# Loading the second attention's first keys one stage earlier

## The chip, the cores and the metric

The kernel runs on one core of a Trainium2 chip. Its metric is the device time of one execution in microseconds, the median of several. Five engines work side by side, each through its own list of instructions in order: TensorE (PE; its weight loads are listed as PEld), VectorE (DVE), ScalarE (ACT), GpSimd (POOL) and SyncE (SP), which here issues nearly all DMA transfers. They wait for one another by semaphores only.

## The reference, cut to what matters

Two layers, each with a cross-attention and a mixture of experts, each added to x. x has 4 x 256 tokens of 256 numbers:

```python
x = x + L0_xattn(layernorm(x), ctx, pos, ...)      # 32 heads of 8, rotary
x = x + L0_ffn(layernorm(x), ...)                  # 16 experts, 2 a token, and a shared one
x = x + L1_xattn(layernorm(x), ctx, ...)           # 16 heads of 16, normed q and k
x = x + L1_ffn(layernorm(x), ...)                  # 60 experts, 4 a token, and a shared one

# in L1_xattn:
q = ln((x @ Wq + bq).reshape(b, s1, H, HD), qn_w, qn_b)
k = ln(kv[..., :HD], kn_w, kn_b)                   # from ctx alone: it does not depend on x
p = softmax(einsum('bhqd,bhkd->bhqk', q, k) * SCALE)
# in L0_ffn:
routed = sum over e of combine[:, e] * (relu(x @ w_up[e]) ** 2 @ w_down[e])
```

The keys of the second attention come from the context, so they can be made before x is there; the queries can't.

## The kernel before, in words

The stages follow each other and are parted by barriers of all engines: preparation and first attention (to 194 us of the profiled span), first experts (to 370 us), second attention (to 494 us), routing and shared expert of the second layer, then its routed experts with a ring of weight slots, then the sum and the store.

**The expert stage** (`route_and_experts_l0`) runs 32 passes n: 16 experts for the first 512 tokens, then the same 16 for the other 512. In each pass TensorE computes the hidden values of pass n+1 (L1041), then the outputs of pass n (L1052); ScalarE applies Relu (L1245), GpSimd squares (L1141), VectorE weighs and adds to `xs` (L1392, four tiles). The outputs of pass n wait for the square of pass n, the square for the Relu. SyncE loads the weights of one expert into one of four slots after the outputs that read it (L1427).

Between these, in chosen passes, each engine works for the second attention. All keys and the queries of the first 512 tokens are projected, normalised, turned and split into three bf16 parts whose sum is the fp32 number. ScalarE makes the first part (`high`, L1457), VectorE the remainder (`rest`, L1467), ScalarE the second part (`mid`, L1477), VectorE the third (`low`, L1486). SyncE writes the parts to stacks in DRAM (`split_writes`, L233; three transfers a split). The four key splits are written behind the expert loads of passes 20, 21, 23 and 24 (`KEYS_WRITTEN`), the two query splits behind the last pass. In passes 28 and 29 the code reads, on ScalarE and on VectorE:

```python
if n == 28:
    for s in Q_SPLITS[0:2]: high(s)     # VectorE: rest(s)
if n == 29:
    for s in Q_SPLITS[0:2]: mid(s)      # VectorE: low(s)
```

In each pass ScalarE's Relu stands ahead of these, and on VectorE the four additions of the pass do. In passes 2, 5, 8, 11, 14 and 17 SyncE also loads weights of two experts of the second layer into the first half of its ring: `ew13` (0.7 MB) and the down weights `ew2` (`load_weights`, L1760). The second half of the ring is loaded in the routing stage.

**The second attention** (`attention` with `L1`) goes through 8 units of 8 heads. A unit needs a side of keys and a side of queries, 96 rows of 8 x 256 bf16 numbers, 384 KB each, loaded from the stacks by `load_side` (L469) into one of four buffers, and rows of ones under the keys, loaded by GpSimd (`load_ones`, L488). `load_first_units` loads the first four units at the start of the stage, key side and query side in turn; one semaphore for each buffer counts both sides, and the first scores of a unit (L629) wait for it. Ahead of the loop, scores and maxima (L769) of two units run, in between the same query work for the last 512 tokens (`LateQueries`), which starts on VectorE with the norm of four tiles (L157 to L165).

Of the kernel before, what the change touches and what calls it, by code (L numbers as in the profile page):

```python
# [14 lines left out]
BF16 = mybir.dt.bfloat16  # L15
# [194 lines left out]
SB = 4  # L210
KEYS_WRITTEN = (20, 21, 23, 24)
SPLIT_BANKS = (6, 7, 0, 1)
SPLIT1_BANKS = (6, 7, 6, 7, 6, 7, 6, 7)
# [702 lines left out]
def route_and_experts_l0(nc, m, io):  # L916

    with ExitStack() as ctx:
# [42 lines left out]
        def _(sp):  # L961
# [19 lines left out]
            for n in range(UNITS0 - WSLOTS):  # L981
                sp.wait_ge(e_down_ps, 4 * (n + 1))
                load_expert_l0(sp, m, io, (n + WSLOTS) % E0, n % WSLOTS)
                if n % 3 == 2 and n // 3 < PAIRS:
                    load_weights(sp, m, io, n // 3 * 2)
                if n in KEYS_WRITTEN:
                    written(KEYS_WRITTEN.index(n))
            for s in Q_SPLITS[0:2]:
                written(s)
# [116 lines left out]
        @block.gpsimd  # L1106
        def _(pool):
            nc.gpsimd.memset(ctxT_dca[:], 0.0).then_inc(ctx_step, 1)
            pool.wait_ge(ctx_step, 1)
# [35 lines left out]
        def _(act):  # L1145
# [67 lines left out]
            def queries(n):  # L1213
# [20 lines left out]
                if n == 28:  # L1234
                    for s in Q_SPLITS[0:2]:
                        high(s)
                if n == 29:
                    for s in Q_SPLITS[0:2]:
                        mid(s)
# [10 lines left out]
        def _(dve):  # L1250
# [96 lines left out]
            def queries(n):  # L1347
# [32 lines left out]
                if n == 28:  # L1380
                    for s in Q_SPLITS[0:2]:
                        rest(s)
                if n == 29:
                    for s in Q_SPLITS[0:2]:
                        low(s)
# [247 lines left out]
def load_first_units(nc, m, io, block):  # L1633

    lay = L1
    part_dma = m.part_dma[lay.name]

    @block.sync
    def _(sp):
        for a in range(SB):  # L1640
            sp.wait_ge(part_dma[a], 16 * WRITES)
        load_side(sp, m, lay, m.ks1, "k", m.loaded1, 0, 0)
        for a in range(2):
            sp.wait_ge(part_dma[a], 2 * 16 * WRITES)
        load_side(sp, m, lay, m.qs1, "q", m.loaded1, 0, 0)
        for u in range(1, UNIT_BUFS[lay.name]):
            load_side(sp, m, lay, m.ks1, "k", m.loaded1, u, u)
            load_side(sp, m, lay, m.qs1, "q", m.loaded1, u, u)

    @block.gpsimd  # L1650
    def _(pool):
        load_ones(pool, m, io, lay, m.ks1)

# [99 lines left out]

def load_weights(eng, m, io, b):

    w13, w2, s = ring_slot(m, b)
    sem = m.ew_loaded[b % RING // 2]
    for w, dram in ((w13, "L1_w13"), (w2, "L1_w2")):
        eng.dma_start(w[:, s:s + 2, :, :].rearrange("p a c n -> p a (c n)"), io[dram][b:b + 2, :, :].rearrange(  # L1760
            "a p n -> p a n")).then_inc(sem, 16)
# [32 lines left out]
def route_shared_l1(nc, m, io, block, ctx):  # L1794
# [45 lines left out]
    def _(sp):  # L1840
# [15 lines left out]
        sp.wait_ge(xn_ready, NT)  # L1856
        sp.dma_start(m.x_rows.rearrange("(i p) d -> p i d", p=P), m.xn[:]).then_inc(m.x_sent, 16)
        for q in range(PAIRS, RING // 2):
            load_weights(sp, m, io, 2 * q)
# [484 lines left out]
def build(nc, io, out):  # L2344
    with ExitStack() as ctx:
# [12 lines left out]
        m.ew13 = m.sb("ew13", [P, EARLY, KD, 2 * I1])  # L2358
        m.ew2 = m.sb("ew2", [HCP, EARLY, 2, D])
        m.ew_loaded = [m.sem(f"ew_loaded{j}") for j in range(RING // 2)]  # L2360
# [11 lines left out]
        with ExitStack() as scope:  # L2372
# [14 lines left out]
            m.old_sems, m.stage_sems = m.stage_sems, []  # L2387
            with ExitStack() as early:
                m.qw = m.sb("qw", [P, KD + 1, D], ctx=early)
                with ExitStack() as layer:  # L2390
# [6 lines left out]
                with ExitStack() as stage:  # L2397
                    m.qs1, m.ks1 = (m.sb(n, stack_shape(L1), BF16, stage) for n in ("l1_qs", "l1_ks"))
                    m.loaded1 = [m.sem(f"l1_loaded{b}", stage) for b in range(UNIT_BUFS[L1.name])]
                    with nc.Block() as block:  # L2400
# [75 lines left out]
```

## Time and profile before

| what | us |
|---|---|
| median of 3 runs (762.67 to 765.81) | 764.84 |
| the profiled execution's own time | 768.52 |
| its span, first to last instruction | 766.6 |
| expert stage, barrier to barrier | 193.9 to 370.1 |
| second attention, barrier to barrier | 370.1 to 494.4 |
| TensorE busy in the span | 646.2 |
| VectorE busy | 425.9 |
| ScalarE busy | 297.3 |
| GpSimd busy | 259.2 |

Times on the trace's line count from the first instruction of the span. A busy share is a mean over stages with different limits, so each stage is read by itself: who waits, and for whom.

### The profile page before, as it was taken

Reading aid. Unit: us, or ns where it says so; the run is one execution under the profiler, and the core shown is the slowest. Engines: PE = TensorE matmul, PEld = TensorE weight load, DVE = VectorE, ACT = ScalarE, POOL = GpSimd, SP = SyncE. Lnnn points to the kernel's source line nnn. Section 1 sums busy time; section 2 is a strip of 40 time slices with the busy share of each in tenths; the row PEclk is TensorE's granted clock in tenths of the full one; section 3 lists DMA queues with packets and bytes.
Section 4 is the critical chain, followed back from the end, with each engine's and each line's share of the span. In section 5 each row is a group of like instructions: output and inputs, shape, how many; then the busy total and the mean of one; then the engine's idle time right before and its main releaser. Section 6 shows DMA issues by size and latency. Waiting matters only on the chain. (4 is left out here: it accounts for less than half of the span.)

```text
span 766.6 us, 12462 instructions
## 1 busy us (share of the span) xinstructions
PE 646.2 (84%) x4224; PEld 388.7 (51%) x4224; DVE 425.9 (56%) x1130; ACT 297.3 (39%) x552; POOL 259.2 (34%) x403
## 2 busy tenths in 40 slices
PE   1657988887799999999569999599999999999750
PEld 1542444444566666676335556365666555555330
DVE  4668788863330767967687564448982222222116
ACT  1332777785323122423036667342214232232110
POOL 5350011111135323313101333302258677777140
PEclk9895899998599999999779999759999999999875
DMA  3086122100600464553914310099001899999907
GB/s 116 1 277 197 45 64 64 45 2 1 175 0 1 127 182 151 166 179 97 240 32 126 85 45 2 12 276 245 4 12 36 236 290 276 271 269 279 266 32 274
DMA packets 82615, 99.59 MB, mean 130 GB/s; under 512 B 11610, under 2 KB 58049, under 8 KB 82547
## 3 DMA queue, kind: packets, MB, share of 16 engines
q1 hardware_dynamic: 74738, 86.53, 39.9%
q0 software_dynamic: 5600, 8.53, 4.3%
q10 hardware_dynamic: 2208, 3.67, 1.3%
q8 instruction: 36, 0.59, 0.3%
q14 instruction: 33, 0.26, 0.1%
HBM read 82.42 MB, written 21.63 MB: 136 GB/s over the span
## 5 line engine op out<-in xcount | busy, mean ns | idle before, releaser
L769 DVE TENSOR_REDUCE l_mx<-ps 128x2 f32<-128x512 f32 (+2 forms) x256 | 125.9, 550 | 46.7 <-PE ps L629 46.4
L857 ACT ACTIVATE l_prob<-ps 128x1024 f32<-128x1024 f32 x96 | 98.4, 1026 | 27.0 <-PE ps L659 26.8
L629 PE MATMUL ps<-l_ks,l_qs 48*128 48x256 bf16 (+1 forms) x384 | 73.1, 305 | 26.4 <-DMA l_qs<-l_q_stacks 13.2
L1392 DVE SCALAR_TENSOR_TENSOR xs<-ps,comb,xs 128x256 f32<-128x256 f32 x128 | 55.8, 482 | 59.5 <-PE ps L1052 59.4
L674 PE MATMUL ps<-l_prob,v 128*9 128x256 f32 (+1 forms) x768 | 71.4, 395 | 1.1 <-ACT l_prob L857 1.1
L2146 POOL DMA_INDIRECT y_rows<-r_sw,row x53 | 53.4, 1008 | 44.3 <-DVE r_sw L2287 33.6
L2280 DVE TENSOR_TENSOR r_hot<-r_hot,ps 128x352 f32<-128x352 f32 (+1 forms) x35 | 15.1, 432 | 95.1 <-ACT r_hot L2255 95.1
L1141 POOL TENSOR_TENSOR r_ehid<-r_erelu 128x512 f32<-128x512 f32 x32 | 35.5, 1109 | 83.6 <-ACT r_erelu L1245 83.5
L1790 POOL DMA_INDIRECT xg<-x_rows,r_empty x53 | 56.2, 1060 | 19.9 <-issue 10.5
L1052 PE MATMUL ps<-f_w,r_ehid 128*128 128x256 f32 x256 | 60.8, 381 | 0.2
L1041 PE MATMUL ps<-xT,f_w 128*128 128x512 f32 x128 | 60.0, 593 | 0.0
L629 PEld LDWEIGHTS ps<-l_ks,l_qs 48*128 48x128 bf16 (+1 forms) x384 | 30.1, 103 | 58.0 <-issue 21.8
L1052 PEld LDWEIGHTS ps<-f_w,r_ehid 128*128 128x128 f32 x256 | 48.5, 190 | 21.0 <-issue 13.9
L659 PE MATMUL ps<-l_qs,l_ks 50*128 50x256 bf16 (+1 forms) x384 | 57.6, 285 | 0.0
L597 POOL TENSOR_TENSOR attn<-rest,l_rec 128x32 f32<-128x32 f32 x64 | 14.4, 246 | 115.0 <-DVE l_rec L788 115.0
L597 POOL TENSOR_TENSOR l_ctxv<-rest,l_rec 128x64 f32<-128x64 f32 x64 | 17.6, 296 | 84.6 <-DVE l_rec L788 84.6
L2255 ACT ACTIVATE r_hot<-ps 128x352 f32<-128x352 f32 (+1 forms) x35 | 13.7, 392 | 79.8 <-PE ps L2184 79.8
L1874 PE MATMUL ps<-xT,r_sw 128*128 128x512 f32 x88 | 42.2, 621 | 0.0
L2287 DVE TENSOR_SCALAR r_sw<-ps,row_w 128x256 f32<-128x256 f32 x53 | 24.0, 481 | 30.1 <-PE ps L2205 30.1
L674 PEld LDWEIGHTS ps<-l_prob,v 128*9 128x9 f32 (+1 forms) x768 | 27.2, 99 | 23.4 <-issue 10.2
L2184 PE MATMUL ps<-ew,r_at_low 128*64 128x352 f32 (+1 forms) x304 | 38.3, 465 | 0.1
L2184 PE MATMUL ps<-ew13b,r_at_low 128*64 128x352 f32 (+1 forms) x240 | 33.3, 478 | 5.4 <-DMA ew2b<-in_L_w 5.4
(278 smaller groups left out, 1110.4 us busy)
## 6 DMA issues: line engine op xcount, KB each, us to landing
ew<-in_L_w SPq DMA_DIRECT2D x18, 704.0 KB, 8.1
ew13b<-in_L_w SPq DMA_DIRECT2D x12, 704.0 KB, 10.9
f_w<-in_L_w SPq DMA_DIRECT2D x32, 256.0 KB, 2.7
ew<-in_L_w SPq DMA_DIRECT2D x18, 384.0 KB, 9.8
ew2b<-in_L_w SPq DMA_DIRECT2D x12, 384.0 KB, 13.9
ew13b<-in_L_w SPq DMA_DIRECT2D x12, 352.0 KB, 13.1
l_k_stacks<-part SPq DMA_DIRECT2D x8, 384.0 KB, 3.3
l_ks<-l_k_stacks SPq DMA_DIRECT2D x32, 96.0 KB, 2.2
```

Source lines behind the costliest of these rows:

```text
L629: ins = nc.tensor.matmul(ps[:, score_bank(n) + k, qt * S:(qt + 1) * S], qs[row:row + R, u % NBUF, col, qt * P:(qt + 1) * P], ks[row:row + ...
L659: ins = nc.tensor.matmul(ps[:, 2 + 2 * (n % 2) + k, kt * S:(kt + 1) * S], ks[row:row + lay.krows, b, col, kt * P:(kt + 1) * P], qs[row:row ...
L674: ins = nc.tensor.matmul(ps[row:row + W, 6, (c % 2) * S:(c % 2 + 1) * S], v[:, n // UP // GR * QT + kt, head, :], prob[:, n % PROBS, k, kt ...
L769: ins = nc.vector.reduce_max(mx[:, u % 2, :, s, head], one[:, :, lo:hi], AX_X)
L857: nc.scalar.activation(prob[:, n % PROBS, :, :, :].rearrange("p h k q -> p (h k q)"), ps[:, 2 + 2 * (n % 2):4 + 2 * (n % 2), :].rearrange( ...
L1041: ins = nc.tensor.matmul(m.ps[:, n % 2, :], m.f0_up[:, n % WSLOTS, c, :], m.xT[:, c, half * HT:(half + 1) * HT], start=(c == 0), stop=(c = ...
L1052: nc.tensor.matmul(m.ps[:, 2 + t, 0:D], ehid[:, n % 2, t * P:(t + 1) * P], m.f0_down[:, n % WSLOTS, :], start=True, stop=True).then_inc(e_ ...
L1392: v.scalar_tensor_tensor(m.xs[:, i, :], m.ps[:, 2 + t, 0:D], m.comb[:, i, e:e + 1], m.xs[:, i, :], ALU.mult, ALU.add).then_inc(e_added, 1)
L1790: nc.gpsimd.indirect_dma_start(m.xg[:, b % XBUF, :], None, m.x_rows, bass.IndirectOffsetOnAxis(m.token[:, b:b + 1], 0), bounds_check=T - 1 ...
L1874: ins = nc.tensor.matmul(ps[:, 2 * (q % 2) + a, :], sw13[:, k, own], m.xT[:, k, h * TILES * P:(h + 1) * TILES * P], start=(k == 0), stop=( ...
L2146: nc.gpsimd.indirect_dma_start(m.y_rows, bass.IndirectOffsetOnAxis(m.row[:, b:b + 1], 0), yb[:, b % YBUF, :], None, bounds_check=ROWS - 1, ...
L2184: ins = nc.tensor.matmul(ps[row:row + n, spot(b), 0:2 * I1], xgT[:, spot(b), c * P + row:c * P + row + n], w13[:, s, c, :], start=(c == 0) ...
```

## The change

Four edits go together.

- The key buffers of the second attention (`ks1`) no longer have a place of their own: they lie over the down weights of the first ring half (`ew2`, widened from 96 to 128 partitions; a partition's size is unchanged), which the second attention doesn't read.
- So the down weights of the first half are loaded later: in the expert stage only `ew13` (part 0) is loaded, and the six loads of `ew2` (part 1) go to the routing stage, behind the second layer's input and ahead of the ring's second half.
- The first four key sides are loaded in the expert stage, behind the expert load of pass 26 and after a wait for all key writes; the ones are loaded by GpSimd at the head of that stage. `load_first_units` loads only the four query sides.
- `mid` and `low` of the first two query splits move from pass 29 to pass 28.

```diff
+KEYS_LOADED = 26
@@ expert stage, SyncE
                 if n % 3 == 2 and n // 3 < PAIRS:
-                    load_weights(sp, m, io, n // 3 * 2)
+                    load_weights(sp, m, io, n // 3 * 2, 0)
                 if n in KEYS_WRITTEN:
                     written(KEYS_WRITTEN.index(n))
+                if n == KEYS_LOADED:
+                    for a in range(SB):
+                        sp.wait_ge(part_dma[a], 16 * WRITES)
+                    for u in range(UNIT_BUFS[L1.name]):
+                        load_side(sp, m, L1, m.ks1, "k", m.loaded1, u, u)
@@ expert stage, GpSimd
         def _(pool):
+            load_ones(pool, m, io, L1, m.ks1)
             nc.gpsimd.memset(ctxT_dca[:], 0.0).then_inc(ctx_step, 1)
@@ expert stage, ScalarE (VectorE: rest, low)
                 if n == 28:
                     for s in Q_SPLITS[0:2]:
                         high(s)
-                if n == 29:
                     for s in Q_SPLITS[0:2]:
                         mid(s)
@@ load_first_units
     def _(sp):
-        for a in range(SB):
-            sp.wait_ge(part_dma[a], 16 * WRITES)
-        load_side(sp, m, lay, m.ks1, "k", m.loaded1, 0, 0)
         for a in range(2):
             sp.wait_ge(part_dma[a], 2 * 16 * WRITES)
-        load_side(sp, m, lay, m.qs1, "q", m.loaded1, 0, 0)
-        for u in range(1, UNIT_BUFS[lay.name]):
-            load_side(sp, m, lay, m.ks1, "k", m.loaded1, u, u)
+        for u in range(UNIT_BUFS[lay.name]):
             load_side(sp, m, lay, m.qs1, "q", m.loaded1, u, u)
-    @block.gpsimd
-    def _(pool):
-        load_ones(pool, m, io, lay, m.ks1)
@@ load_weights
+    both = ((w13, "L1_w13"), (w2, "L1_w2"))
+    for w, dram in both if part is None else both[part:part + 1]:
@@ routing stage, SyncE
         sp.dma_start(m.x_rows.rearrange("(i p) d -> p i d", p=P), m.xn[:]).then_inc(m.x_sent, 16)
+        for q in range(PAIRS):
+            load_weights(sp, m, io, 2 * q, 1)
         for q in range(PAIRS, RING // 2):
             load_weights(sp, m, io, 2 * q)
@@ build
-        m.ew2 = m.sb("ew2", [HCP, EARLY, 2, D])
+        m.ew2_all = m.sb("ew2", [P, EARLY, 2, D])
+        m.ew2 = m.ew2_all[0:HCP]
+                rows, bufs, own, _ = stack_shape(L1)
+                m.ks1 = m.ew2_all[:].rearrange("p s c n -> p (s c n)").bitcast(BF16)[0:rows, 0:bufs * own * S].rearrange(
+                    "p (b g t) -> p b g t", b=bufs, g=own)
+                m.loaded1 = [m.sem(f"l1_loaded{b}", early) for b in range(UNIT_BUFS[L1.name])]
```

## Rows read from the trace of the kernel before

**Rows 1.** The page's groups, L1041: count, busy, mean ns, idle before.

```profile
L1041 PE MATMUL ps<-xT,f_w 128*128 128x512 f32 x128 | 60.0, 593 | 0.0
```

**Rows 2.** Timeline at the handover: start, us, engine, line, operation, [idle before, releaser].

```profile
370.18 0.38 DVE L157 BATCH_NORM_AGGREGATE mv<-bn 128x2 f32<-128x6 f32 x4 [0.30 <-PEq L918]
370.26 0.33 SPq L469 DMA_DIRECT2D l_ks<-l_k_stacks  x1
370.57 2.09 POOL L488 DMA_DIRECT2D l_ks<-in_l_ones  x4 [4.57 <-POOLq L918]
370.68 0.49 SPq L469 DMA_DIRECT2D l_qs<-l_q_stacks  x1
...
372.05 1.66 DVE L165 TENSOR_SCALAR xn<-xs,mv,rstd 128x256 f32<-128x256 f32 x4
...
377.14 1.03 PE L629 MATMUL ps<-l_ks,l_qs 96*128 96x256 bf16 x4 [9.09 <-DMA l_qs<-l_q_stacks]
...
377.78 1.42 DVE L769 TENSOR_REDUCE l_mx<-ps 128x2 f32<-128x480 f32 x4 [4.08 <-PE ps L629]
```

**Rows 3.** The key buffers' instructions, 360 to 410 us: the loads' landing.

```profile
DMA to landing us min/median/max: 4.6/5.3/7.5
```

**Rows 4.** Timeline of the expert stage's last passes.

```profile
357.40 0.60 ACT L1245 ACTIVATE r_erelu<-ps 128x512 f32<-128x512 f32 x1 [0.71 <-PE ps L1041]
...
358.07 1.04 POOL L1141 TENSOR_TENSOR r_ehid<-r_erelu 128x512 f32<-128x512 f32 x1 [3.19 <-ACT r_erelu L1245]
...
359.53 1.40 DVE L1467 SCALAR_TENSOR_TENSOR rest<-ps,norm_T,part 128x512 f32<-128x512 f32 x2
...
360.31 1.38 ACT L1477 ACTIVATE part<-rest,norm_T 128x512 bf16<-128x512 f32 x2 [2.31 <-DVE rest L1467]
...
360.64 1.89 PE L1052 MATMUL ps<-f_w,r_ehid 128*128 128x256 f32 x8
...
362.37 1.88 PE L1041 MATMUL ps<-xT,f_w 128*128 128x512 f32 x4
...
364.09 3.96 PE L1052 MATMUL ps<-f_w,r_ehid 128*128 128x256 f32 x16
...
364.96 1.04 POOL L1141 TENSOR_TENSOR r_ehid<-r_erelu 128x512 f32<-128x512 f32 x1 [1.67 <-ACT r_erelu L1245]
366.05 1.59 PEld L1052 LDWEIGHTS ps<-f_w,r_ehid 128*128 128x128 f32 x8 [0.48 <-POOL r_ehid L1141]
```

**Rows 5.** Timeline of SyncE's queue alone, 343 to 381 us.

```profile
347.92 7.21 SPq L1427 DMA_DIRECT2D f_w<-in_L_w  x3
363.86 3.86 SPq L233 DMA_DIRECT2D l_q_stacks<-part  x6
```

**Rows 6.** DMA issues, 318 to 400 us: count, KB each, median us to landing.

```profile
f_w<-in_L_w SPq DMA_DIRECT2D x10, 256.0 KB, 2.6
l_k_stacks<-part SPq DMA_DIRECT2D x4, 384.0 KB, 3.6
```

**Rows 7.** Windows in the routing stage: last columns PEclk, DMA share, GB/s.

```profile
532.00:536.00 4.00, 4.00 (x12) 2.01 (x11) 3.90 (x4) 0.34 (x1) 1.42 (x1) 1.00 0.93 229
536.00:540.00 4.00, 4.00 (x17) 2.76 (x16) 3.79 (x9) 1.62 (x4) 1.27 (x1) 1.00 0.13 42
```

**Rows 8.** DMA issues, 405 to 500 us, the later units' query sides.

```profile
l_qs<-l_q_stacks SPq DMA_DIRECT2D x4, 384.0 KB, 3.9
```

**Rows 9.** Waits, 195 to 370 us: total, times, longest.

```profile
POOL v L1118 <- DMA r_vb<-in_L_vb_T: 14.2, 1, 14.2
```

**Rows 10.** Timeline of the routed experts, the first use of `ew2`.

```profile
593.23 1.90 PE L2205 MATMUL ps<-ew,r_hot 88*64 88x256 f32 x16
```

**Rows 11.** The window behind the expert stage: PEclk third from the end.

```profile
371.00:372.00 1.00, 0.00 (x0) 0.00 (x0) 0.65 (x4) 0.20 (x1) 1.00 (x3) 0.63 0.49 103
```

**Rows 12.** A window at the start of the expert stage, same columns.

```profile
211.00:212.00 1.00, 1.00 (x2) 0.45 (x2) 0.91 (x4) 0.00 (x0) 0.85 (x5) 0.50 0.00 0
```

**Rows 13.** Timeline there: matmuls of the form of L1041.

```profile
208.93 6.31 PE L1001 MATMUL ps<-xT,r_sup 128*128 128x512 f32 x8
```

More of the change, by code:

```diff
@@ L1382, in queries @@
                         rest(s)
-                if n == 29:
                     for s in Q_SPLITS[0:2]:
@@ L1752, in slot_starts, with load_weights @@
     return np.stack([whole, rest, BASE * P - FULL - whole - rest]).astype(np.float32)
-def load_weights(eng, m, io, b):
+def load_weights(eng, m, io, b, part=None):
     w13, w2, s = ring_slot(m, b)
     sem = m.ew_loaded[b % RING // 2]
-    for w, dram in ((w13, "L1_w13"), (w2, "L1_w2")):
+    both = ((w13, "L1_w13"), (w2, "L1_w2"))
+    for w, dram in both if part is None else both[part:part + 1]:
         eng.dma_start(w[:, s:s + 2, :, :].rearrange("p a c n -> p a (c n)"), io[dram][b:b + 2, :, :].rearrange(
@@ L2397, in build @@
                 with ExitStack() as stage:
-                    m.qs1, m.ks1 = (m.sb(n, stack_shape(L1), BF16, stage) for n in ("l1_qs", "l1_ks"))
-                    m.loaded1 = [m.sem(f"l1_loaded{b}", stage) for b in range(UNIT_BUFS[L1.name])]
+                    m.qs1 = m.sb("l1_qs", stack_shape(L1), BF16, stage)
                     with nc.Block() as block:
```

## The prediction

> **What bounds the kernel now.** I read the page's span first, then the chain of stages around the change. Only two places matter: the last passes of the expert stage, and the handover from it to the second attention. The profiled span is 766.6 us; that execution took 768.52 us, 3.7 us above the 764.84 us median of the three runs (762.67 to 765.81). Every sum below is a difference on the profiled time line, and I put it on the median: the stretch that changes is 20 us long and has no reason to differ between the two.
>
> The expert stage is bound by TensorE. The first matmuls of its passes, 128 in all, had 0.0 us of idle time in front [rows 1]: whatever makes TensorE wait there lengthens the kernel one for one. The handover is bound by a load. The barrier lets the engines go at 370.18 us, SyncE issues the first keys at 370.26, the first queries at 370.68, and TensorE starts its scores at 377.14, released by the queries after 9.09 us of idleness [rows 2]. VectorE meanwhile normalises its four late tiles until 372.05 + 1.66 = 373.71 us, then sits idle for 4.08 us until the maxima at 377.78 [rows 2]. So at most 4.08 us can be gained before VectorE is the bound. The queries took 6.4 us from issue (370.68) to landing (377.1) [rows 2], the quickest keys 4.6 us and the slowest 7.5 [rows 3]: eight sides of 384 KB lay in the queue together with four small loads of ones.
>
> **The change, part by part.**
>
> *1. The query splits end one pass sooner.* This moves ScalarE's two `mid` from pass 29 to the end of pass 28, and VectorE's two `low` likewise. ScalarE works in order. In pass 28 it will do Relu(28), `high` twice, then `mid` twice, and only then Relu(29). `mid` waits for `rest`, and `rest` stands on VectorE behind the four additions of pass 28. In the trace `rest` runs from 359.53 for 1.40 us and `mid` follows it at 360.31 for 1.38 us, ending at 361.69 [rows 4]. None of that comes sooner, since the additions it stands behind don't. But Relu(29), which ran at 357.40 [rows 4], now starts at 361.7 us. Behind it is queued everything ScalarE has left in the stage; the one who waits is GpSimd's square, and through it TensorE.
> Step by step: Relu(29) ends at 361.7 + 0.6 = 362.3; the square follows a Relu by 0.07 us (357.40 + 0.60 to 358.07 for this one), takes 1.04 us, and TensorE loads weights 0.05 us behind it (364.96 + 1.04 = 366.00 to 366.05 for the last one) [rows 4]. So the second matmuls of pass 29 start at 362.3 + 0.07 + 1.04 + 0.05 = 363.46 us. They ran at 360.64, right behind the first matmuls of pass 30 [rows 4]. TensorE's next instructions are behind these second matmuls in its own order, so nothing fills the gap: it idles from about 360.8, for 2.65 us, and everything behind it, the first matmuls of pass 31 (362.37 now) and its square (364.96 now) [rows 4], moves by 363.46 - 360.64 = 2.8 us. The additions, the statistics and the barrier hang on that tail: **+2.8 us**, barrier at 373.0. The bounds are narrow, 2.5 to 3.1, as every duration stands in the rows.
> What it buys: the query writes, which began at 363.86 and took 3.86 us to issue [rows 5], begin about 2 us sooner. They were no bound before: the queries were issued 0.50 us after the barrier, and until 370.59 SyncE was issuing keys [rows 2]. So it is worth 0.1 us at most.
>
> *2. The first keys are loaded in the expert stage.* Behind the expert load of pass 26 SyncE now waits for the key writes and issues four loads of 384 KB. The writes were issued well before the three expert loads that start at 347.92 [rows 5] and land in 3.6 us [rows 6]; the second of the three comes some 3.5 us later, at about 351.4, so there is nothing left to wait for. Queued behind on SyncE is the last expert load, until now at 347.92 + 7.21 - 0.33 = 354.8 or so. Its weights are read at 362.37 now, at 365.2 then. Four sides are 1.57 MB; at the 229 GB/s of a busy stretch [rows 7] that is 6.9 us, so with 2.6 us of its own [rows 6] it lands by about 351.8 + 6.9 + 2.6 = 361.3. Covered, with 3.9 us to spare; **0**. If that cover were gone, each us of lateness would be a us of the stage.
> At the handover only the four query sides are left, and the first is first in the queue. Its landing is not in the trace of before. The nearest row is the same transfer first in line with one other side behind it: 3.9 us [rows 8]; below it lies an expert load of 256 KB with 2.6 us, above it the queries' own 6.4 us [rows 2, 6]. I take 3.9, the same transfer. Then scores start at 373.08 + 3.9 + 0.06 = 377.0 us, which is 4.0 us behind the barrier, where it was 377.14 - 370.18 = 6.96: **-2.9 us** (-4.2 to -0.4). VectorE is free at 373.71 + 2.8 = 376.5, so it isn't late first.
>
> *3. The ones.* GpSimd's four issues of 2.09 us [rows 2] move to the head of the expert stage. There GpSimd waits 14.2 us for a small load [rows 9]; its three short copies in front of that wait have the same cover. **0**; it would cost up to 2.1 if that wait went.
>
> *4. The down weights.* Six loads, each of two experts with 96 rows of 512 numbers of 4 bytes, 0.39 MB, leave the expert stage, where no engine waited for them, and go ahead of the second half of the weight ring in the next stage, on SyncE. 2.36 MB at 229 GB/s are 10.3 us. The queue ran dry between 536 and 540 us [rows 7], so it runs dry near 548; the first matmul that reads down weights is at 593.23 [rows 10]. **0**, 45 us of cover.
>
> Clears of four more semaphores on VectorE in the tail of the second attention lie in its wait for TensorE, which hides them; were it gone, they would cost their own length. **Sum:** +2.8 - 2.9 = -0.1 us. From the bounds of the load: -1.4 to +2.4.
>
> **A rule that speaks against it.** After the expert stage's last matmul the granted clock was at its upper level until a mean of 0.63 between 371 and 372 us [rows 11]. TensorE's last matmul ended at 364.09 + 3.96 = 368.05 [rows 4]; a mean of 0.63 in that one us puts the fall near 371.3, 3.2 us later. The Trainium skill, page "TensorE: Matmul & The Clock Gate", section "Part 1: The HAM clock gate", says that a monitor of recent activity puts an idle TensorE back to half rate. By it the new gap could cost more than its length. The trace shows that behind the stage, where the work had ended for good; it shows no fall in a stop like the new one, of 2.65 us between full stretches, so for that it neither agrees nor differs. The sum by it stands among the rivals.
>
> **Rivals.**
> - *The clock falls in the new gap* (slower than before). The place is passes 29 to 31. Eight matmuls of the first kind took 6.31 us at 0.50 of the clock [rows 12, 13]; at the upper level four of that form take 1.88 [rows 4], so the factor is 1.68. Four groups at 1.72 us (360.64 to 362.37 [rows 4]) are left behind the gap: 4 x 1.72 x 0.68 = +4.7, net +4.6, 769.4 us. It decides if the clock falls before TensorE starts again. Against it: behind the stage the clock fell only after 3.2 us without a matmul. 7%.
> - *The queries land no sooner*: four sides still share the queue, 6.4 us as before. Net +2.8 - 0.4 = +2.4, 767.2 us. For it: all sides of that stretch took long, even the quickest keys 4.6 [rows 3]. Against: 3.9 with one side behind. 13%.
> - *ScalarE's order costs nothing* because something I missed lets Relu(29) through or covers it. Then the barrier stays at 370.18, queries land at 374.2: -2.9, 761.9 us. Against it: the code's order and 0.0 us of slack. 9%.
> - *The key loads hold the expert loop up*: the load of pass 26 shares with them and takes the 7.5 us of the slowest side [rows 3], so its weights come at 358.9, just as they are needed; up to +2, 766.7 us. 5%.
> - *It gains more than its delay*: -2.9 with no delay and the clock still at its upper level when scores begin. Under 761.0. 4%.
>
> **How the numbers follow.** The forecast (-1.4 to +1.0) has 62%. About 0.5%, 3.8 us, is what a measurement of this kernel can tell from no change. Only the clock rival goes beyond it upward, and the last one downward: faster 0.05, same 0.86, slower 0.09. Predicted: 764.84 - 0.1 = 764.7 us. For 8 in 10 the range takes in the bounds of the load, the two rivals at 761.9 and 767.2, and a little of the runs' own scatter: 761.6 to 768.0.
>
> **What the profile will show.** Right: Relu(29) starts behind `mid`, near 361.7 on this time line; TensorE idles some 2.6 us ahead of the second matmuls of pass 29; barrier near 373.0; first query side lands in about 3.9 us; scores near 377.0; VectorE's idleness in front of its maxima down from 4.08 to under 1.5 us. Wrong if the gap isn't there, if the clock falls in it, if the query side takes over 5 us, or if an expert matmul waits for its weights.

## The result and the profile after

The changed kernel is **slower**, by some 1.1%. Its median is 770.65 us (769.72 to 775.44, 6 runs) against 763.81 us (758.82 to 770.26, 6 runs) for the kernel before in the same comparison; the ratio is 1.0114, interval 1.0068 to 1.016. The forecast was 764.7 us, no change, in a range that ended at 768.0. The profiled execution of after took 771.26 us, its span is 769.4 us. (Of the ratios below, that of e2 leaves out as slow four of its twelve runs, 772.33 to 775.08, counted from one low run of 759.11; the mean of all twelve is 768.99 against 765.48 for before.)

The two spans differ by only 2.8 us, because the profiled execution of before was 2.65 us longer ahead of the expert stage, where nothing is changed: over all fourteen profiles of this study that part takes 191.4 to 194.1 us without any order. So I compare stretches. Each begins and ends at an instruction that both kernels have (VectorE's first aggregate of a stage, the first scores, the first maxima, ScalarE's first exponential), and its length is the difference of two starts on the timeline.

| stretch, us | before | after | difference |
|---|---|---|---|
| expert stage to its barrier | 176.08 | 180.20 | +4.1 |
| barrier to first maxima | 7.60 | 6.35 | -1.25 |
| first maxima to first exponential | 24.15 | 25.25 | +1.1 |
| first exponential to routing stage (the attention loop and its tail) | 92.63 | 94.62 | +2.0 |
| routing stage to the end | 272.04 | 271.53 | -0.5 |

The third line is not the change's: in kernels that carry all, some or nothing of it that stretch lies between 23.8 and 25.3 us (25.0 in e10, which has nothing of it). What has to be explained is the first, the second and the fourth line.

**The end of the expert stage.** Timeline of after, all engines' rows for the last passes; they answer [rows 4] and [rows 5]. Columns: start, us, engine, line, operation, idle before and its releaser.

```profile
356.02 1.88 PE L1047 MATMUL ps<-xT,f_w 128*128 128x512 f32 x4
...
357.40 1.38 ACT L1482 ACTIVATE part<-rest,norm_T 128x512 bf16<-128x512 f32 x2 [3.62 <-DVE rest L1472]
...
358.69 1.06 ACT L1251 ACTIVATE r_erelu<-ps 128x512 f32<-128x512 f32 x2
359.00 3.87 SPq L234 DMA_DIRECT2D l_q_stacks<-part  x6
359.34 2.19 POOL L1148 TENSOR_TENSOR r_ehid<-r_erelu 128x512 f32<-128x512 f32 x2 [7.37 <-ACT r_erelu L1251]
360.59 3.40 PE L1058 MATMUL ps<-f_w,r_ehid 128*128 128x256 f32 x8 [2.69 <-POOL r_ehid L1148]
363.83 1.88 PE L1047 MATMUL ps<-xT,f_w 128*128 128x512 f32 x4
```

ScalarE writes the middle parts (L1482) first and only then does the Relu of pass 29 (L1251, two of them back to back). GpSimd's square follows, and TensorE, which had stopped at 357.90, starts its second matmuls of pass 29 at 360.59. That is the forecast gap. But those matmuls took 3.40 us, where the same group took 1.89 in [rows 4]. Windows of after over the same time; PEclk is third from the end:

```profile
357.00:360.00 3.00, 0.90 (x3) 0.07 (x1) 2.44 (x4) 2.35 (x4) 0.66 (x1) 1.00 0.41 100
360.00:361.00 1.00, 0.41 (x1) 0.41 (x2) 0.00 (x0) 0.00 (x0) 1.00 (x2) 0.53 1.03 345
361.00:363.50 2.50, 2.50 (x7) 1.94 (x7) 0.97 (x2) 0.00 (x0) 0.53 (x1) 0.50 1.03 338
363.50:366.00 2.50, 2.50 (x10) 1.44 (x9) 0.96 (x2) 0.25 (x1) 0.00 (x0) 1.00 0.43 145
```

The granted clock fell from its upper level (2.4 GHz, 1.00) to the lower one (1.2 GHz, 0.50) near 360.06 (a mean of 0.53 from 360 to 361), 0.5 us before TensorE started again, stayed there for that one group, and was back for the next. From the start of the first matmuls of pass 30 to those of pass 31 after took 363.83 - 356.02 = 7.81 us; twice 1.72, that is 3.44, is the full pace [rows 4]. The loss is 4.37 us: 2.85 of waiting and 1.51 of half clock.

**The expert stage's matmuls as groups.** Page of after, answering [rows 1]: the first matmuls still had no idle time in front, so the key loads held nobody up; the second ones now have 2.9 us.

```profile
L1058 PE MATMUL ps<-f_w,r_ehid 128*128 128x256 f32 x256 | 62.3, 387 | 2.9 <-POOL r_ehid L1148 2.7
...
L1047 PE MATMUL ps<-xT,f_w 128*128 128x512 f32 x128 | 60.0, 592 | 0.0
```

**The handover.** Timeline of after, answering [rows 2]:

```profile
371.65 0.38 DVE L157 BATCH_NORM_AGGREGATE mv<-bn 128x2 f32<-128x6 f32 x4 [0.30 <-PEq L919]
371.67 4.59 SPq L470 DMA_DIRECT2D l_qs<-l_q_stacks  x4
...
373.51 1.38 DVE L165 TENSOR_SCALAR xn<-xs,mv,rstd 128x256 f32<-128x256 f32 x4
...
377.35 1.04 PE L630 MATMUL ps<-ew,l_qs 96*128 96x256 bf16 x4 [7.84 <-DMA l_qs<-l_q_stacks]
...
378.00 1.32 DVE L770 TENSOR_REDUCE l_mx<-ps 128x2 f32<-128x480 f32 x3 [3.11 <-PE ps L630]
```

The queries are issued 0.02 us behind the barrier, and TensorE starts 5.68 us later, still released by them. VectorE's idleness ahead of the maxima went from 4.08 to 3.11 us.

**The attention loop.** Two rows of the DMA page and one of the waits, 405 to 495 us, first of before and then of after. The first column block of the queue's row is packets, MB and the share of 16 engines' time; a load's row ends with its median landing; the wait's row has total, times and longest.

```profile
q1 hardware_dynamic: 8336, 4.83, 18.8%
...
l_ks<-l_k_stacks SPq DMA_DIRECT2D x4, 384.0 KB, 4.6
...
PE ps L629 <- DMA l_ks<-l_k_stacks: 3.0, 3, 1.7
```

```profile
q1 hardware_dynamic: 8352, 4.84, 20.1%
...
ew<-l_k_stacks SPq DMA_DIRECT2D x4, 384.0 KB, 4.9
...
PE ps L630 <- DMA ew<-l_k_stacks: 4.2, 3, 1.9
```

The same bytes in as many packets keep the DMA engines busy 7% longer (20.1 to 18.8), the key sides land 0.3 us later, and TensorE waits 1.2 us more for them. No step of the prediction speaks of this.

### The profile page after: what moved, and what is told of

It reads as the page before. It is cut to its first block and busy times, and to the rows that moved or that the text cites. A ratio compares the mean times of both kernels' runs of the same rounds, so it can differ in the third digit from the quotient of the medians.

```text
span 769.4 us, 12462 instructions
## 1 busy us (share of the span) xinstructions
PE 644.2 (84%) x4224; PEld 387.8 (50%) x4224; DVE 425.2 (55%) x1130; ACT 297.1 (39%) x552; POOL 259.5 (34%) x403
## 5 line engine op out<-in xcount | busy, mean ns | idle before, releaser
L1047 PE MATMUL ps<-xT,f_w 128*128 128x512 f32 x128 | 60.0, 592 | 0.0
L630 PE MATMUL ps<-l_ks,l_qs 48*128 48x256 bf16 x256 | 46.6, 302 | 13.6 <-DVE l_mx L770 9.5
L630 PE MATMUL ps<-ew,l_qs 96*128 96x256 bf16 x128 | 26.0, 306 | 13.7 <-DMA l_qs<-l_q_stacks 7.8
L660 PE MATMUL ps<-l_qs,l_ks 50*128 50x256 bf16 x256 | 37.2, 285 | 0.0
```

Of the source, the lines that this page charges most:

```text
L630: ins = nc.tensor.matmul(ps[:, score_bank(n) + k, qt * S:(qt + 1) * S], qs[row:row + R, u % NBUF, col, qt * P:(qt + 1) * P], ks[row:row + ...
L1047: ins = nc.tensor.matmul(m.ps[:, n % 2, :], m.f0_up[:, n % WSLOTS, c, :], m.xT[:, c, half * HT:(half + 1) * HT], start=(c == 0), stop=(c = ...
```

## The experiments

All twelve kernels in one table, each beside the kernel before on its own chip. "Pass" is the time from the first matmuls of pass 30 to those of pass 31; "scores" is from the barrier to the first scores; "key" is the median landing of a key side in the loop and "wait" TensorE's total wait there; "loop" is the fourth line of the table above.

| kernel | pass | scores | key | wait | loop | median us | ratio, interval |
|---|---|---|---|---|---|---|---|
| before | 3.44 | 6.96 | 4.6 | 3.0 | 92.6 | | |
| after | 7.81 | 5.70 | 4.9 | 4.2 | 94.6 | 770.65 | 1.0114 (1.0068 to 1.016) |
| e1 | 3.44 | 5.77 | 4.9 | 4.9 | 94.9 | 765.55 | 1.0002 (0.9967 to 1.0037) |
| e2 | 8.02 | 7.44 | 4.6 | 3.0 | 91.4 | 769.86 | 1.0009 (0.9964 to 1.0054) |
| e3 | 7.81 | 5.26 | 5.0 | 5.0 | 94.9 | 769.59 | 1.0057 (1.0027 to 1.0088) |
| e4 | 3.44 | 5.26 | 5.0 | 3.6 | 93.5 | 766.51 | 1.0026 (0.9992 to 1.0059) |
| e5 | 3.50 | 5.70 | 4.8 | 3.5 | 93.5 | 764.49 | 0.9978 (0.9946 to 1.0009) |
| e6 | 3.44 | 6.21 | 5.1 | 5.3 | 95.2 | 762.23 | 0.9944 (0.9912 to 0.9976) |
| e7 | 3.44 | 5.77 | 4.9 | 4.3 | 93.1 | 763.31 | 0.9966 (0.9938 to 0.9994) |
| e8 | 3.44 | 6.23 | 5.1 | 4.3 | 94.3 | 761.3 | 0.9933 (0.991 to 0.9956) |
| e9 | 3.45 | 5.97 | 4.6 | 3.2 | 93.1 | 762.2 | 0.9967 (0.9933 to 1.0001) |
| e10 | 3.45 | 7.46 | 4.7 | 3.8 | 92.3 | 766.07 | 1.004 (1.0009 to 1.0071) |
| e11 | 3.45 | 4.51 | 4.5 | 3.2 | 92.1 | 759.75 | 0.9933 (0.9896 to 0.9969) |
| e12 | 6.87 | 5.43 | 4.8 | 3.7 | 93.9 | 769.8 | 1.0071 (1.0037 to 1.0104) |

**e1 and e2: each part alone.** e1 is after with `mid` and `low` back in pass 29:

```diff
                 if n == 28:
                     for s in Q_SPLITS[0:2]:
                         high(s)
+                if n == 29:
                     for s in Q_SPLITS[0:2]:
                         mid(s)
...
+                if n == 29:
                     for s in Q_SPLITS[0:2]:
                         low(s)
```

> The changed kernel with mid and low of the query splits back in pass 29: only the keys, the ones and the down weights are moved. Theory A (Relu(29) behind mid is what costs): no gap ahead of the second matmuls of pass 29, no fall of the clock there, barrier as in the kernel before; the first query side lands some 5.6 us after its issue, scores about 1.3 us sooner than before: -1 to -2 us against the kernel before. Theory B (the moved loads or the buffers laid over the down weights cost): still +4 to +7 us against the kernel before.

e2 is the kernel before with the same two lines taken out.

> The kernel before with mid and low in pass 28 and nothing else changed. Theory A: the gap of 2.7 us ahead of the second matmuls of pass 29, the clock at its lower level in it or right behind it, barrier 2.8 to 4.4 us later, scores later by as much: +3 to +7 us. Theory B: 0 to +3 us, the plain delay without anything behind it.

The pass takes 3.44 us in e1 and 8.02 us in e2: the whole loss of the expert stage belongs to the first part. One row of e2, its second matmuls of pass 29; the gap is the same 2.69 us, the half-clock group 3.66 us:

```profile
361.79 3.66 PE L1052 MATMUL ps<-f_w,r_ehid 128*128 128x256 f32 x8 [2.69 <-POOL r_ehid L1141]
```

In time, e2's ratio can't be told from 1, and its mean over all twelve runs is 3.5 us above before. e1, which has all the rest of the change, equals before: the handover's 1.2 us are there (scores 5.77 against 6.96), and the loop, 94.9 us, gives them back.

**e12: the gap filled.** To part the 4.37 us into waiting and clock, TensorE gets work in the gap, ahead of its wait, into a bank that the next matmuls overwrite. The work's result is read by nobody.

```diff
             def routed_outputs(n):
+                if n == 29:
+                    pe.wait_ge(e_added, 4 * n - 3)
+                    for c in range(4):
+                        nc.tensor.matmul(m.ps[:, 2, :], m.f0_up[:, (n + 1) % WSLOTS, c % KD, :],
+                                         m.xT[:, c % KD, HT:2 * HT], start=True, stop=True)
                 pe.wait_ge(e_hid_done, n + 1)
```

> The kernel after, with four more matmuls in pass 29 on TensorE ahead of its wait for the hidden layer: 128x512 outputs into a bank that the next matmuls overwrite, some 2.3 us of work whose result nobody reads. They fill the 2.7 us gap and nothing waits for them. Theory (of the 4.4 us, 2.8 are the wait itself and 1.5 the clock that falls at its end): granted clock 1.00 through the gap and behind it, the matmuls of pass 29 take 1.9 us instead of 3.4, start of the expert stage to the barrier 178.7 us (after: 180.2), time 1.5 us under the kernel after. Rival (the 1.5 us are something else, or the four matmuls come too late and hold what follows): 180 us or more, time as after or above.

Timeline of e12 on TensorE, and below it one window with its PEclk:

```profile
356.69 1.88 PE L1047 MATMUL ps<-xT,f_w 128*128 128x512 f32 x4
358.40 3.60 PE L1055 MATMUL ps<-xT,f_w 128*128 128x512 f32 x8
361.84 1.89 PE L1063 MATMUL ps<-f_w,r_ehid 128*128 128x256 f32 x8
363.56 1.88 PE L1047 MATMUL ps<-xT,f_w 128*128 128x512 f32 x4
```

```profile
360.00:362.00 2.00, 2.00 (x6) 0.92 (x5) 0.30 (x1) 0.42 (x1) 2.00 (x2) 1.00 0.71 240
```

With work in the gap the clock stays at its upper level and the second matmuls take 1.89 us again. So the 1.51 us are the clock, which falls with the gap and doesn't without it. My filling was too long: each matmul counts as two rows, so the four took 3.60 us, not 2.3, and held the next group about 0.6 us. The pass is 0.94 us shorter than in after (7.81 - 6.87) = 1.51 - 0.57. The barrier came only 0.2 us sooner than in after (180.00), as the passes ahead of the gap had taken 0.7 us longer, and the time, 1.0071 of before, can't tell the 0.9 us.

**e7: the splits as early, nothing held.** Only the order on the two engines is changed against after: `rest` ahead of VectorE's additions of pass 28, `low` behind them, `mid` behind the Relu of pass 29.

```diff
+                if n == 29:
                     for s in Q_SPLITS[0:2]:
                         mid(s)
...
                 if n == 28:
                     for s in Q_SPLITS[0:2]:
-                        rest(s)
-                    for s in Q_SPLITS[0:2]:
                         low(s)
...
                 half, e = n // E0, n % E0
+                if n == 28:
+                    for s in Q_SPLITS[0:2]:
+                        rest(s)
```

> As the kernel after, with three steps of the query splits set elsewhere in passes 28 and 29: VectorE forms the remainder ahead of its additions of pass 28, forms the lowest part behind them, and ScalarE writes the middle part behind its Relu of pass 29. The splits end as soon as in the kernel after or sooner, and the Relu of pass 29 no longer stands behind the middle part. Theory gap (the 4.4 us of the first part are the wait ahead of the second matmuls of pass 29 and the clock that falls at its end): the 2.7 us gap is gone, the granted clock stays at 1.00 there, start of the expert stage to the barrier 175.9 us (after: 180.2), and the time is 4 us under the kernel after, equal to e1, about 766. Rival (the additions of passes 28 and 29 or the later middle part now end last): 177 us or more to the barrier, a wait on VectorE's or GpSimd's step in place of the gap, at most 2 us under the kernel after.

Timeline of e7; the fence's rows are of ScalarE, TensorE and SyncE:

```profile
355.23 0.60 ACT L1252 ACTIVATE r_erelu<-ps 128x512 f32<-128x512 f32 x1 [0.71 <-PE ps L1047]
355.72 1.32 ACT L1484 ACTIVATE part<-rest,norm_T 128x512 bf16<-128x512 f32 x2
...
356.75 1.88 PE L1047 MATMUL ps<-xT,f_w 128*128 128x512 f32 x4
358.13 3.86 SPq L234 DMA_DIRECT2D l_q_stacks<-part  x6
358.47 1.89 PE L1058 MATMUL ps<-f_w,r_ehid 128*128 128x256 f32 x8
360.19 1.88 PE L1047 MATMUL ps<-xT,f_w 128*128 128x512 f32 x4
```

The Relu is first, `mid` behind it, TensorE has no gap, and the expert stage takes 176.6 us (before 176.1, after 180.2). Yet the query writes begin 9.9 us ahead of the barrier (358.13 to 368.01), 6.3 in before: the splits do end sooner here, without holding anything. The theory of the gap holds. e7 came out at 0.9966 of before, some 2.7 us under what e1's ratio had let me expect; the intervals of the two overlap.

**e3 and e4: why the first queries are late.** In e3, after's SyncE waits for the first query side before it issues the other three; e4 has the same on e1.

```diff
         for u in range(UNIT_BUFS[lay.name]):
             load_side(sp, m, lay, m.qs1, "q", m.loaded1, u, u)
+            if u == 0:
+                sp.wait_ge(m.loaded1[0], 32)
```

> The changed kernel, but SyncE waits until the first query side has landed before it issues the other three. If the four sides share the DMA engines (the first landed after 5.6 us, when about three sides had moved), it lands in about 3.1 us and scores come 2.4 us sooner than in the changed kernel, until VectorE's norm is the bound: about +5 us against the kernel before, where the changed kernel has +7. If the 5.6 us are the load's own latency, no change: +7.

> Both edits: mid and low back in pass 29, and the first query side alone in the queue. If both theories hold: scores 3.0 to 3.7 us sooner than in the kernel before, then VectorE's norm is the bound; -3 to -4 us against the kernel before. If the latency is the load's own, as the kernel with only the splits put back: -1 to -2 us.

Alone in the queue the first side landed 0.4 us sooner, after 5.2 us, where 3.1 had been expected. The landings of e3's first side (issued at 371.02) and of its second (at 376.24, into the queue the first had left empty):

```profile
DMA to landing us min/median/max: 5.2/5.2/5.2
...
DMA to landing us min/median/max: 3.9/3.9/3.9
```

Two transfers of the same size and form into an empty queue, 5.2 us apart in time: 5.2 and then 3.9 us (in e4 5.2 and 4.4). So most of it is not the sides behind it. Windows of e3 (last columns DMA share and GB/s), then a row of its DMA page for 372 to 373 us, and last the same row of e11 for 371 to 372 us:

```profile
373.00:373.50 0.50, 0.00 (x0) 0.00 (x0) 0.50 (x2) 0.00 (x0) 0.00 (x0) 0.57 1.08 327
...
375.00:375.50 0.50, 0.00 (x0) 0.00 (x0) 0.00 (x0) 0.00 (x0) 0.00 (x0) 0.50 0.07 20
```

```profile
q8 instruction: 1, 0.02, 10.0%
```

```profile
q8 instruction: 1, 0.02, 6.9%
```

**e5, e6, e9 and e10: why the key sides land later.** The buffer they load into begins, over the down weights, at an address 32 bytes past a multiple of 64 (77,088 in the program's allocation); the key buffers of before began at a multiple of 256 (188,672). e5 is e1 with the overlay 32 bytes further on (a multiple of 64), e9 is e1 with it 224 bytes further on (a multiple of 256):

```diff
-                ...bitcast(BF16)[0:rows, 0:bufs * own * S]...
+                ...bitcast(BF16)[0:rows, 16:16 + bufs * own * S]...      (e5)
+                ...bitcast(BF16)[0:rows, 112:112 + bufs * own * S]...    (e9)
```

e6 is e1 with unused buffers of 32 bytes ahead of the early expert weights and behind them, which puts up weights, down weights and key stacks at multiples of 64, and moves everything allocated behind them by 64 bytes, the second attention's query buffers among it:

```diff
+        m.sb("pad0", [P, 8])
         m.ew13 = m.sb("ew13", [P, EARLY, KD, 2 * I1])
         m.ew2_all = m.sb("ew2", [P, EARLY, 2, D])
         m.ew2 = m.ew2_all[0:HCP]
+        m.sb("pad1", [P, 8])
```

> As e1 (the key stacks of the second attention over the down weights, the query splits in the pass where they were before), but the key stacks begin 32 bytes further into that buffer: in every kernel so far with the overlay they began at an address that is 32 bytes past a multiple of 64, in the kernel before at a multiple of 64. Theory address: the key sides of the attention loop land 0.3 us later in the overlay (4.9 in e1, 4.6 in the kernel before, median) because of where in a 64-byte line they begin; here the median is 4.6 again, TensorE waits for key sides in the loop some 3.0 us in sum (e1: 4.9), first exponential to start of the routing stage 92 to 93 us (e1: 94.9), and the time is 1 to 2 us under the kernel before. Theory place (rival: it is the buffer's place or the earlier load, not its start in the line): landing stays 4.8 to 5.0, the loop 94 to 95 us, the time that of e1, equal to the kernel before.

> As e1, with 32 unused bytes ahead of the early expert weights and 32 behind them, so that the early up weights, the early down weights and with them the key stacks all begin at a multiple of 64 bytes and nothing else changes its remainder. Theory address: key landing 4.6 as in e5, and the early weights of the routed stage land sooner too, if anything waits for them there: 1 to 2 us under the kernel before, as e5 or up to 1 us lower. Theory place: as e1, equal to the kernel before within 0.5 us.

My first form of the theory fell: at a multiple of 64 the landing stayed at 4.8 and 5.1 us. But e6 said more. It moved the query buffers from 172,288, a multiple of 256, to 64 bytes past one, and the query sides became slower too. Its DMA rows, 405 to 495 us:

```profile
q1 hardware_dynamic: 8306, 4.82, 21.2%
...
l_qs<-l_q_stacks SPq DMA_DIRECT2D x4, 384.0 KB, 4.2
ew<-l_k_stacks SPq DMA_DIRECT2D x4, 384.0 KB, 5.1
```

So the next pair asks for the multiple of 256. e10 is the opposite test: the kernel before, nothing of the change in it, with its key buffers 64 bytes further on.

```diff
-                    m.qs1, m.ks1 = (m.sb(n, stack_shape(L1), BF16, stage) for n in ("l1_qs", "l1_ks"))
+                    m.qs1 = m.sb("l1_qs", stack_shape(L1), BF16, stage)
+                    m.sb("pad0", [P, 16], F32, stage)
+                    m.ks1 = m.sb("l1_ks", stack_shape(L1), BF16, stage)
+                    m.sb("pad1", [P, 48], F32, stage)
```

> As e1, but the key stacks begin 224 bytes into the down weights' buffer, at a multiple of 256 bytes. A start at a multiple of 64 alone left the landing of the key sides at 4.8 us (e5) and, where the query buffers moved by 64 bytes, raised theirs from 3.9 to 4.2 (e6). Theory (it is the start against a multiple of 256 bytes, as the key and query buffers of the kernel before had): key sides land in 4.6 us again, TensorE waits for them in the loop about 3.0 us in sum (e1: 4.9), first exponential to routing stage 92 to 93 us, time 1 to 2 us under e1. Rival (the buffer's place, or queries loaded in another rhythm): 4.8 to 5.0, loop 94 to 95, time as e1.

> The kernel before, whose key buffers of the second attention begin 64 bytes later (64 bytes past a multiple of 256), everything behind them as before. Nothing else of the change. Theory (the start): key sides land in 4.9 us (before: 4.6), the loop takes 1 to 2 us longer, time 1 to 2 us above the kernel before. Rival: landing 4.6 and the kernel before's time.

The rows of e9 and then of e10, same views:

```profile
l_qs<-l_q_stacks SPq DMA_DIRECT2D x4, 384.0 KB, 3.8
ew<-l_k_stacks SPq DMA_DIRECT2D x4, 384.0 KB, 4.6
...
PE ps L630 <- DMA ew<-l_k_stacks: 3.2, 4, 1.4
```

```profile
q1 hardware_dynamic: 8639, 4.92, 20.0%
...
l_ks<-l_k_stacks SPq DMA_DIRECT2D x4, 384.0 KB, 4.7
...
PE ps L629 <- DMA l_ks<-l_k_stacks: 3.8, 4, 1.3
```

At a multiple of 256 the overlay's key sides land in 4.6 us as before, the waits fall from 4.9 to 3.2 us and the loop from 94.9 to 93.1. e10 goes the expected way, but only a third as far: landing 4.6 to 4.7, waits 3.0 to 3.8, time 1.004 of before (1.0009 to 1.0071), and its loop, 92.3 us, is not longer at all. The packet records of the traces show the loads themselves, without the loop's scatter. The mean time of the load queue's 512-byte packets, nearly all of them pieces of key and query sides, over 405 to 495 us:

| where the sides begin | kernels | mean of a 512-byte packet, ns |
|---|---|---|
| both at a multiple of 256 bytes | before, e2, e9, e11 | 30.0 to 30.2 |
| keys 64 bytes past one | e5, e10 | 32.1, 31.9 |
| keys 32 bytes past one | after, e1, e3, e4, e7, e12 | 32.6 to 33.3 |
| keys and queries 64 bytes past one | e6, e8 | 36.2, 35.0 |

That the address slows the loads is shown both ways; what it costs the loop is some 1 us of waits, and the rest of the fourth line's 2 us I can't tell from scatter (kernels with the overlay off the multiple: 93.1 to 95.2 us; the others, but for e10: 91.4 to 93.1).

**e8 and e11: the parts put together.** e8 is e7's order with e6's addresses. e11 is e7's order with the unused buffers of 224 and 32 bytes, so that the early weights and the stacks over them begin at multiples of 256.

```diff
+        m.sb("pad0", [P, 56])
         m.ew13 = m.sb("ew13", [P, EARLY, KD, 2 * I1])
...
+        m.sb("pad1", [P, 8])
```

> The order of e7 and the addresses of e6 together. If both theories hold, to the barrier 175.9 us, the first scores 5.7 us behind it, the loop 92 to 93 us: 2 to 3 us under the kernel before, some 762 to 763. If only the theory on the gap holds: equal to the kernel before. If neither: as the kernel after, 5 us above the kernel before.

> The order of e7, with the early expert weights and the key stacks over them at multiples of 256 bytes (the query buffers and the first attention's buffers keep theirs). Theory: as e7 with key sides landing in 4.6 and query sides in 3.9 (e8: 5.1 and 4.1), 1 to 2 us under e7 on the same chip: about 4 us under the kernel before. Rival: as e8, landing 4.9 to 5.1, 4 to 5 us under the kernel before by the expert weights alone.

Both **beat the two kernels**: 0.9933 of before, some 5 us. e11 has what each theory asks for: pass 3.45, scores 4.51, key sides 4.5, loop 92.1. But the theories don't account for all of the 5 us. In these profiles the stretch from the routing stage to the end took 263.4 us in e8 and 266.7 in e11, where before took 272.0, and nothing was meant to change there (the last section comes back to it).

## Why the prediction was wrong

*The gap of the first part* was right to a tenth: 2.69 us forecast as 2.65, for the reason given, Relu(29) behind `mid`, and in three kernels.

*The step that failed first is the clock in that gap.* It stood among the rivals at 7%, with "behind the stage the clock fell only after 3.2 us without a matmul" against it. In after it fell 2.2 us behind the last matmul, inside a stop of 2.69 us, and all three kernels with the gap show a group at half clock behind it. One row of a fall was read as a bound, and it isn't one. The rival's price was mis-sized in turn: it put four groups at half clock (+4.7); it was one group, +1.51. The Trainium skill, page "TensorE: Matmul & The Clock Gate", section "Part 1: The HAM clock gate", which the prediction quoted and set at 7%, has a monitor of recent activity lower an idle TensorE's clock. The trace now agrees with it, for a stop of 2.69 us.

That the trace of before "shows no fall in a stop like the new one" was read from one place. In its routed experts TensorE waited 3.00 us for weights (a wait of 1.91 us had ended 1.4 us ahead of it), and the clock fell 0.2 us into that stop; and in those of e11 it waited 3.35 us and the clock stayed up through the stop and behind it. The row behind each stop, with one window inside it (PEclk third from the end), before and then e11:

```profile
719.00:720.00 1.00, 0.19 (x2) 0.00 (x0) 0.27 (x1) 0.46 (x1) 0.00 (x0) 0.71 1.07 260
722.19 2.62 PE L2184 MATMUL ps<-ew13b,r_at_low 128*64 128x352 f32 x8 [3.00 <-DMA ew2b<-in_L_w]
```

```profile
714.00:715.00 1.00, 0.00 (x0) 0.00 (x0) 0.00 (x0) 0.00 (x0) 0.00 (x0) 1.00 1.11 281
716.00 1.40 PE L2184 MATMUL ps<-ew13b,r_at_low 128*64 128x352 f32 x8 [3.35 <-DMA ew2b<-in_L_w]
```

So the length of a stop alone doesn't say whether the clock falls; all three kernels with this gap paid for it.

*The second failed step is the query side's landing*, -2.9 in the sum from 3.9 us, "the same transfer" of the loop. It landed in 5.6 us and the handover gave 1.25 us; the scores' start came 1.7 us later than forecast. The bounds of -4.2 to -0.4 held it. e3 shows that the transfer does take 3.9 us in that stage (4.4 in e4), but only 5 us into it.

*The third is a term that was not there*: the key buffer's new address. The prediction followed the loads, their queue and who waits, and costed the buffer's move at nothing without saying so. It costs 1.2 us of waits, up to 2.0 of loop. Here a page would have helped. The Trainium skill, page "DMA: Bandwidth & Descriptors", section "How a descriptor splits into AXI transactions", says that a descriptor is split into transactions that start at multiples of 256 bytes, and that one starting elsewhere pays for bytes that it doesn't use. It tells this of bytes that are fetched; here it is the end that is written. An estimate by that page for pieces of 512 bytes starting 64 bytes past is 18 beats in place of 16, +12.5%, or +6% where only the key half starts there. The packets of e5 and e10, with the key half there, took 6% longer, as estimated; those of e8 and e6, with both halves, 16 and 20%, which is more. For 32 bytes past, the page's arithmetic gives 17 beats, an estimate of +3% with the key half alone; the packets took 8 to 10% longer. So the trace agrees that a start off the multiple costs, and the size by beats is mostly too small.

*The clears* were said to lie in VectorE's wait for TensorE. VectorE's row in the loop's tail, before and then after:

```profile
492.45 0.42 DVE L801 TENSOR_TENSOR xs<-xs,ps 128x256 f32<-128x256 f32 x1 [4.89 <-PE ps L197]
```

```profile
495.90 0.42 DVE L802 TENSOR_TENSOR xs<-xs,ps 128x256 f32<-128x256 f32 x1 [5.23 <-issue]
```

The idle time is 0.33 us longer in after. Which releaser the profile names doesn't tell: it is TensorE in some kernels and VectorE's own issue in others, with the clears moved or not. But the length does: 5.23 us in all eleven kernels that carry the four more clears, 4.89 in all three that don't (before, e2, e10), so the clears had no cover left.

*What held:* the key loads in the expert stage hold nobody (0.0 us ahead of L1047), and the ones and the down weights cost nothing that shows. TensorE's matmuls on the early down weights had 0.7 us of idle time in front in both kernels, ended by ScalarE and not by a load. That routing stage to end is the same within 0.5 us is luck: in the kernels that leave the weights where they are this stretch took between 267.8 and 274.2 us.

The sum by stretches, with what each term was forecast to be: +4.1 (2.8), -1.25 (-2.9), +2.0 (0). That is +4.9 where -0.1 was forecast, and the medians differ by 6.8 with an interval of some 5 to 12 us; the 1.1 us ahead of the first exponential are scatter that happens to add.

## What to carry to other kernels

An instruction moved forward on an in-order engine is worth nothing if it takes the wait of its own operand with it: move the operand's step first (e7), and reckon, for a new stop of TensorE, with the group behind it at half clock. A buffer that is laid over another one inherits its address: look at where it begins before you cost the move at zero, and take the landing of a load at a stage's start from a load at a stage's start.

## What the runs showed of the hardware

- The **start of a buffer** sets the pace of loads of 512-byte pieces into it: a packet took 30.0 to 30.2 ns with both sides at multiples of 256 bytes, 32.6 to 33.3 with the key side 32 bytes past one, 35.0 and 36.2 with both sides 64 past. During the handover, where the DMA engines were busy throughout, the windows of one us from 373 to 378 show 222 to 239 GB/s for e8's queries and 267 to 295 for e11's.
- Whether the same holds for the **weights of the routed experts** is not shown. The weights of the first ring half begin 32 bytes past a multiple of 256 in the kernel before; e6 and e8 move them by 32 bytes, e11 by 224. The mean times are lower with it, by 2.7 us from e5 to e6 and by 1.9 from e7 to e8 (without e7's one run of 771.62), with standard errors of 1.2 and 0.8. But no run changed the weights' address alone: e6 and e8 also put the second half of the ring, 64 bytes further on, at multiples of 256. The rows of the later matmuls of that stage, e7 and then e8:

```profile
L2184 PE MATMUL ps<-ew13b,r_at_low 128*64 128x352 f32 (+1 forms) x240 | 33.1, 477 | 3.6 <-DMA ew2b<-in_L_w 3.6
```

```profile
L2184 PE MATMUL ps<-ew13b,r_at_low 128*64 128x352 f32 (+1 forms) x240 | 31.4, 465 | 0.0
```

  The 477 ns are not a slower matmul for the address: the same matmuls on the early weights, the ones that were moved, take 465 ns in thirteen of the fourteen kernels, before among them. In e7 TensorE waits 3.6 us in all for weights, and one group at half clock follows (2.62 us, where e11's above took 1.40); e8 has no such wait.
- **TensorE's clock** fell in a stop of 2.69 us between full stretches (after, e3) or 0.2 us behind its end (e2), and came back after one group; four matmuls of no use in that stop kept it up (e12). A stop of 3.00 us in the routed experts of before brought it down, one of 3.35 us in e11 left it up.
- **A load at a stage's start** took 1.3 us longer than the same load 5 us later (5.2 and 3.9 us in e3). With four sides in the queue it landed 2.3 to 2.5 us behind the end of a packet of instructions, whenever that came (2.1 to 3.7 us behind the barrier).
